# Writing the negated row maxima ahead of the next pair of maxima in a fused attention and expert kernel

## What is computed

```python
x1t = jnp.swapaxes(x1, 1, 2); x2t = jnp.swapaxes(x2, 1, 2)
q = proj(x1t, Wq, bq); k = proj(x2t, Wk, bk); v = proj(x2t, Wv, bv)
scores = jnp.einsum('bhqd,bhkd->bhqk', q, k) / jnp.sqrt(D_HEAD)
attn = jax.nn.softmax(scores, axis=-1)
out = jnp.einsum('bhqk,bhkd->bhqd', attn, v)
```

## Time and profile before

| | |
|---|---|
| three runs | 1549.8, 1559.02 (median), 1560.58 us |
| the profiled execution | 1560.23 us, of which the span from first to last instruction is 1558.4 us |
| TensorE matmuls (PE) | 1379.7 us busy, 89% |
| TensorE weight loads (PEld) | 649.8 us, 42% |
| VectorE (DVE) | 979.1 us, 63% |
| ScalarE (ACT) | 878.0 us, 56% |
| GpSimd (POOL) | 865.8 us, 56% |

### The profile page before, as it was taken

How to read it: one execution, slowest core, us unless ns; L and a number is a source line. 1 busy time by engine, 2 the same in 40 slices (tenths; PEclk the granted TensorE clock), 3 DMA queues, 4 the chain that set the end, 5 groups by cost and what they waited for, 6 DMA issues and landing times.

```text
span 1558.4 us, 24574 instructions
## 1 busy us (share of the span) xinstructions
PE 1379.7 (89%) x7290; PEld 649.8 (42%) x7290; DVE 979.1 (63%) x1661; ACT 878.0 (56%) x1720; POOL 865.8 (56%) x1278
## 2 busy tenths in 40 slices
PE   3789888888888788888988888889999999999997
PEld 1222222222222222222222222227778888888886
DVE  5777777777777777777777777764665433333332
ACT  1477667666767667666766667663433433333333
POOL 7346656555666657766666655353321455555553
PEclk7799999999999989999999989999999999999999
DMA  5556565556667666666756565535655488886665
GB/s 169 158 166 191 170 179 159 169 165 164 180 156 170 167 148 180 173 163 160 181 151 178 158 156 137 132 90 190 149 138 176 99 207 213 210 180 129 110 112 82
DMA packets 161308, 247.90 MB, mean 159 GB/s; under 512 B 33605, under 2 KB 58828, under 8 KB 161182
## 3 DMA queue, kind: packets, MB, share of 16 engines
q1 hardware_dynamic: 142926, 208.96, 49.0%
q0 software_dynamic: 18256, 37.38, 13.0%
HBM read 141.85 MB, written 103.88 MB: 158 GB/s over the span
## 4 chain that ended last, share of the span: by engine, by line
PE 71%; issue 11%; DVE 7%; DMA 4%; SPq 4%; POOL 2%; ACT 1%; POOLq 1%; DVEq 0%; ACTq 0%
PE m_banks L949 20%; PE bank L877 16%; PE bank L906 16%; PE m_banks L856 8%; PE bank L837 4%; PE bank L882 2%; SPq L470 2%; DVE row_max L1122 2%; PE bank L841 2%; PE bank L893 2%; DMA arena<-pv_d 1%; DVE m_rows L1132 1%; DVE m_rows L1131 1%; POOL xs L780 1%; PE bank L971 1%
## 5 line engine op out<-in xcount | busy, mean ns | idle before, releaser
L1122 DVE TENSOR_REDUCE row_max<-m_banks 128x2 f32<-128x1024 f32 x512 | 617.0, 1220 | 233.1 <-PE m_banks L856 229.4
L1394 ACT ACTIVATE arena<-bank 128x512 f32<-128x512 f32 x1024 | 562.2, 603 | 236.1 <-PE bank L877 235.9
L877 PE MATMUL bank<-arena 112*128 112x512 bf16 x1024 | 330.4, 402 | 129.0 <-DVE m_rows L1132 127.3
L906 PE MATMUL bank<-arena 128*32 128x512 f32 x2048 | 296.1, 652 | 0.2 <-ACT arena L1401 0.2
L877 PEld LDWEIGHTS bank<-arena 112*128 112x128 bf16 x1024 | 80.5, 101 | 400.3 <-DVE m_rows L1132 154.6
L792 POOL DMA_INDIRECT out<-xs,ids x71 | 112.5, 1584 | 173.4 <-ACT xs L1468 137.7
L856 PE MATMUL m_banks<-arena 48*128 48x512 bf16 x1024 | 172.5, 411 | 15.1 <-DVE row_max L1122 8.9
L949 PE MATMUL m_banks<-w_ring,h_hi 128*128 x568 | 183.0, 403 | 0.0
L676 POOL TENSOR_TENSOR arena<-arena 128x512 bf16<-128x512 f32 x62 | 71.5, 1152 | 180.2 <-ACT arena L1386 177.3
L1457 ACT ACTIVATE arena<-m_banks 128x256 f32<-128x256 f32 x103 | 39.5, 384 | 188.9 <-PE m_banks L949 188.8
L949 PE MATMUL m_banks<-w_ring,h_lo 128*128 x284 | 111.7, 393 | 0.0
(11 more groups left out here) (176 smaller groups left out, 2058.3 us busy)
## 6 DMA issues: line engine op xcount, KB each, us to landing
pv_d<-arena SPq DMA_DIRECT2D x32, 512.0 KB, 3.5
w_ring<-split_d SPq DMA_DIRECT2D x60, 256.0 KB
parts_k<-arena SPq DMA_DIRECT2D x96, 128.0 KB
parts_q<-arena SPq DMA_DIRECT2D x96, 128.0 KB
arena<-parts_k SPq DMA_DIRECT2D x64, 192.0 KB
arena<-parts_q SPq DMA_DIRECT2D x64, 192.0 KB
arena<-in_w SPq DMA_DIRECT2D x36, 256.0 KB, 7.3
arena<-in_ctx SPq DMA_DIRECT2D x32, 256.0 KB, 3.4
```

Of the source, the lines that this page charges most:

```text
L877: nc.tensor.matmul(out, k_stack[b % 3][0:SHIFTED, h, kt * P:(kt + 1) * P], q_stack[b % 3][0:SHIFTED, h, :], start=True, stop=True).then_in ...
L906: last = nc.tensor.matmul(pv_ps[2 * DH * j:2 * DH * (j + 1), :], v_ones[b % 3][:, kt, GROUP * g + j, :], probs[pair % 3][:, j, :], start=( ...
L1122: nc.vector.reduce_max(pair, m_ps[(STEPS * b + u) // 2 % M_PAIRS], AX_X).then_inc(s_mx, 1)
L1394: nc.scalar.activation(probs[group % 3][:, j, :], bank_of["scores", b, s], ACT.Exp, scale=float(DH) ** -0.5).then_inc(s_exp, 1)
```

## The change

VectorE issues both rows together, and ahead of the pair of step 4 or 20 in place of behind it. The same instructions run, with the same waits.

```diff
                 for s in range(STEPS):
+                    if s == MAX_AT[1] + 1 and is_b(i):
+                        run(maxima_rows(i, 1))
+                    if s == MAX_AT[0] + 1 and is_b(i + 1):
+                        run(maxima_rows(i + 1, 0))
                     if s % 2 == 0 and is_b(i + 1):
                         maximum(i + 1, s)
-                    if s == MAX_AT[1] + 1 and is_b(i):
-                        begun.append(maxima_rows(i, 1))
                     if s == RECIP_AT and is_b(i - 1):
                         invert(i - 1)
-                    if s == MAX_AT[0] + 1 and is_b(i + 1):
-                        begun.append(maxima_rows(i + 1, 0))
```

## The result

The changed kernel takes 1441.14 us (median of 4 runs, 1437.89 to 1445.13) against 1559.8 us (4 runs, 1549.8 to 1562.36): a ratio of 0.925, 95% interval 0.921 to 0.930, or 118.7 us less. The forecast was 1414 us, so it had the sign, and four fifths of the 145 us that it promised. The profiled execution took 1441.5 us, its span 1439.6 us.

A forecast was written before the change was run, and what follows sets the result against it. TensorE bounds the attention stage, idle 135 of 1000 us. 1560.2 - 127.3 (row waits) + 25 (new waits) - 52 (clock) + 9 (queues) = 1415, so 1414 us, as that execution lies 1.2 above the median; range 1370 to 1475.

The forecast's parts named there:

- The step 4 and step 20 waits go: Attention stage: TensorE's 63 waits of score matmul L877 for the rows (L1132) vanish, 127.3 us.
- New waits behind the reduction of step 22: Step 20 turns with routing: TensorE's second pair of the next group waits for that reduction's buffer, 25 us added.
- the second kind: Step 20s, 6 times, whose two routing instructions take 0.61 and 0.99 us: a new wait of 1.9 us each.
- the case which the prediction told of and did not take: VectorE starts ahead of GpSimd for the second routing instruction: 1.9 becomes about 0.85 us, the sum 6.3 us less.
- The clock: TensorE in the attention stage: five sixths of the 63 us cost of half-clock stretches goes, 52 us.
- The rival by which the waits that are left keep the clock as it was: Attention stage: remaining waits and those behind the reductions keep the clock swinging, no clock gain, 1466 us; chance 0.17.
- Queues: SyncE's queue: late denominators reach TensorE through the rows of step 20, 0.3 us a turn, 9 us added.
- the m_rows wait under 15: Sign in the changed profile: TensorE's wait for m_rows falls from 127 us to under 15.
- the clock at 0.97 or more: Sign in the changed profile: the granted clock of the attention stage, 0.93 before, is 0.97 or more.
- a turn of about 27 us: Sign in the changed profile: a turn of the attention stage, 31 us before, takes about 27.
- idle under 70: Attention stage: the forecast is wrong if TensorE's idle time, 135 us before, stays above 70 us.
- A DMA at the head of the list: Attention stage: the forecast is wrong if a DMA, or ScalarE's exponentials, heads the list of what TensorE waits for.

The follow-up runs named there:

- step 4 alone: Kernel before, with only the rows of step 4 issued together and ahead of the reduction, step 20 as before: 1496.05 us, ratio 0.959.
- step 20 alone: Kernel before, with only the rows of step 20 issued together and ahead of the reduction, step 4 as before: 1487.43 us, ratio 0.956.
- the two faster kernels: Changed kernel with SyncE's three staging DMAs behind the key-part writes: 1426.43 us; the same with denominators also loaded ahead of the two query writes: 1407.53 us.

## Why the prediction was right, and where it was off

**The step 4 and step 20 waits go** (127.3 us): right. 0.3 us is left, the two places split as worked out (51.7 and 73.9 us), and the rows fit into the time in which VectorE waited for TensorE: that wait fell from 229.4 us to 77.5, further than the half that was foretold. VectorE does the same work in a stage that is 120 us shorter, and 40 us more of its waiting is for the denominators (54.4 in place of 14.0).

**New waits behind the reduction of step 22** (25 us): right in kind, and 14.5 us in size. The step that was off is above all the second kind's 1.9 us: 6 x 1.9 = 11.4 us were foretold, four such turns have waits of 0.35 to 0.77 us and two have none, 2.3 us in all, and no wait of L856 is longer than 1.3. One such turn after the change, VectorE and GpSimd:

```profile
258.23 1.29 POOL L717 TENSOR_TENSOR arena<-arena 128x512 f32<-128x512 f32 x1
...
258.92 0.64 DVE L1169 TENSOR_TENSOR route<-route 128x32 f32<-128x32 f32 x1
...
259.59 1.32 POOL L724 TENSOR_TENSOR staged_lo<-arena,staged_hi 128x512 fp32r<-128x512 f32 x1
259.59 0.19 DVE L1170 TENSOR_TENSOR route<-route 128x32 f32<-128x32 f32 x1
```

The first routing instruction is long until GpSimd's L717 ends, as in the earlier trace rows; the second starts with GpSimd's next and takes 0.19 us, where it took 0.99. TensorE waits 0.75 us there. That is the case which the prediction told of and did not take: with nothing between the two instructions VectorE is in time. The Trainium skill, page "SBUF — State Buffer", section "Who interferes with whom", has whichever starts first keep the shared ports. The trace agrees as far as it can tell two starts at 259.59 apart. Of the six turns of this kind five are so; in the sixth the first instruction takes 0.18 us and the second 1.25. The first instruction's length varies (0.18 to 0.66 us in these six), and the wait with it.

**The clock** (52 us, bounds 0 and 63): 38.8 us came back, and the granted clock is 0.98. By the profile's share, 2 x 0.02 x 880 = 35 us at half clock are left where 140 were. The rival by which the waits that are left keep the clock as it was, 1466 us, did not come: 24 waits of L856, at most 1.3 us, are left, and the clock rose. The Trainium skill, page "TensorE: Matmul & The Clock Gate", section "A second HAM failure mode: psum-queue depth-cycling", has short idles between groups of matmuls swing the clock. These did not. Half clock is still found at the long waits, as at 743 us: seen in windows of 1 us, the stage after the change has eight stretches of it, 34 us in all, and each begins within or just behind a wait of L865 for the logits' copy, of 1.6 to 4.4 us.

**Queues** (9 us, bounds 0 and 28): this is the term that failed. "I take a third, 0.3 us a turn" measured 32.5 us of TensorE's time in 20 waits (29.6 more than before), above the upper bound. The first links were the right ones (denominators late, VectorE's reciprocal late, TensorE late); the last was not, since the delay reached TensorE through the logits' copy and L865 and not through the rows of step 20. And it was priced by what VectorE waited for the denominators before, as if that wait had a fixed size. It is what the loop through SyncE's queue is longer than a turn would otherwise be, and grows as turns get shorter: with stages of 1000, 936, 922 and 880 us (before, step 4 alone, step 20 alone, both) VectorE waited 14.0, 27.1, 31.6 and 54.4 us for the denominators. In the chain of the changed kernel seven such loops in a row, from a key-part landing that begins at 349.13 us to one at 552.72, take 29.1 us each; a turn was to take 27. The profile of before had the warning in the queue's own list: 132.0 us of slack in front of the rows, which the prediction did not read.

Against the forecast, then, idle time: L865 +20.6 us (32.5 less the 2.9 of before and the 9), L856 -13.1 (14.5 less 2.6 and 25), the rest +4.6; and the clock +13.2. Together 25 us, which is the miss in the stage (120 against 145). That the total came so near is partly luck: the waits behind the reductions, put 13.1 us too high, hide part of the 20.6.

**What the prediction said would show it:** the m_rows wait under 15 (0.3), the clock at 0.97 or more (0.98), a turn of about 27 us (880 / 32 = 27.5), idle under 70 (53.8): all seen. The wait of L856 was to be some 25 us and is 14.5. "A DMA at the head of the list" was named as a sign against it, and one stands there in disguise. The loop explains the missing idle time: with it shortened, the wait of L865 is 2.1 us, idle is 30, and the time 1407.53, below the forecast. How much of the 13 us of clock the long stalls cost is argued and not shown by itself. The low stretches that are left stand at these stalls; and in the two faster kernels, with the stalls down to 12.3 and 2.1 us, the granted clock over the span is 0.979 and 0.983 against 0.974, which points the same way.

## To carry to other kernels

A wait that an engine makes because another engine does something unneeded first is priced well by a timeline: write down when the data was there, when the reader came, and what stood between. But once a wait that recurs each turn is gone, look for the loop that is next as long as a turn, in the in-order DMA queue first: its waits for other engines are slack that the change will spend. In such a queue, try bulk transfers behind the writes that somebody waits for, do not put a load right behind the store whose landing it needs, and expect that moving one entry ahead makes others later: of the six arrangements of SyncE's transfers tried on the changed kernel, two made it faster, three made it slower, and one was not told apart from it.

## What the chip showed that was not expected

The row DMAs, 4 KB each, took 1.7 us from issue to landing (median) before the change and 2.8 us after it, with the same bytes moved in less time (160 GB/s in the stage before, 182 after). The 128 KB key parts took 5.3 to 8.5 us to land in the chain of the changed kernel, behind three transfers of 256 KB. Neither was a fixed cost. For the key parts a run shows that what stands ahead of them counts: with the three transfers moved behind, their landing stands in the chain in 7 turns in place of 24. For the rows no run changed only what stands ahead of them, and why they took longer is open.
